# Token attention: maximum, shift and exponential over both units of a turn in one instruction each

## The reference, cut to what matters

```
raw    = einsum('bhid,bhjd->bhij', q, k)
scores = sips_alpha * tanh(raw / sips_beta)
scores = scores + lam * hamming + lat          # bilinear terms of the token's tanh codes
scores = where(causal, scores, -inf)
attn   = softmax(scores, axis=-1)
out    = einsum('bhij,bhjd->bhid', attn, v)
```

## Time and profile before

| what | value |
|---|---|
| median of 3 runs | 4054.79 us (4053.88 to 4055.74) |
| the profiled execution | 4051.72 us |
| its span, first to last instruction | 4049.9 us |
| granted TensorE clock, mean | 0.987 |
| busy share of the span | PE 94%, PEld 72%, DVE 74%, ACT 66%, POOL 48% |
| L400, shift, POOL | 384 instructions, 1039 ns each |
| L469, maximum, DVE | 384 instructions, 674 ns each |
| L587, exponential, ACT | 384 instructions, 662 ns each |

### The profile page before, as it was taken

One profiled execution on the slowest core, in us unless ns is written; L12 is line 12 of the kernel. 1 busy time (PEld: TensorE's weight loads), 2 busy tenths in 40 slices (PEclk: granted clock), 3 DMA queues, 4 the chain that ended last, 5 costly groups with the idle time before them and its releaser, 6 DMA issues. The chain is left out here.

```text
span 4049.9 us, 104259 instructions
## 1 busy us (share of the span) xinstructions
PE 3822.8 (94%) x34969; PEld 2917.7 (72%) x34969; DVE 2984.6 (74%) x7049; ACT 2676.5 (66%) x6409; POOL 1939.4 (48%) x1865
## 2 busy tenths in 40 slices
PE   7999999969999989899999889999999999999999
PEld 5666666647777766577777557777777777789998
DVE  6888888869999965799998665555555555566666
ACT  7888888857778853678787336666666666633333
POOL 4666666657777731566666333334333333311111
PEclk9999999979999999999999999999999999999999
DMA  3000000000000001000000110000000000000000
GB/s 105 1 0 0 0 0 0 0 14 20 20 24 20 24 22 27 14 13 16 13 16 18 24 34 2 1 0 0 0 0 0 0 0 0 0 6 9 9 9 9
DMA packets 69052, 47.65 MB, mean 12 GB/s; under 512 B 38360, under 2 KB 57952, under 8 KB 68832
## 3 DMA queue, kind: packets, MB, share of 16 engines
q1 hardware_dynamic: 68960, 46.43, 4.4%
HBM read 12.62 MB, written 4.19 MB: 4 GB/s over the span
## 5 line engine op out<-in xcount | busy, mean ns | idle before, releaser
L1672 ACT ACTIVATE l_probs<-l_act,l_neg_max 128x128 f32<-128x128 f32 (+1 forms) x1024 | 415.5, 425 | 274.0 <-DVE l_neg_max L1629 271.4
L1609 POOL TENSOR_TENSOR l_probs<-l_probs,l_sums 128x512 f32<-128x512 f32 x384 | 391.0, 1039 | 366.1 <-DVE l_sums L1637 366.1
L400 POOL TENSOR_TENSOR t_probs<-t_probs,t_neg_max 128x512 f32<-128x512 f32 x384 | 390.9, 1039 | 298.6 <-DVE t_neg_max L469 298.4
L1629 DVE TENSOR_REDUCE l_neg_max<-l_act 128x2 f32<-128x512 f32 (+1 forms) x384 | 246.9, 684 | 356.3 <-PE l_act L1728 356.3
L1990 ACT ACTIVATE e_hT<-e_act 128x512 f32<-128x512 f32 x256 | 152.8, 597 | 285.3 <-PE e_act L2011 285.3
L459 DVE SCALAR_TENSOR_TENSOR t_probs<-t_tanh_qk,scalars_sb,t_dve 128x512 f32<-128x512 f32 x384 | 269.4, 743 | 83.6 <-ACT t_tanh_qk L569 52.9
L854 POOL TENSOR_TENSOR w_swappedQ<-w_rawQ,w_table 128x512 f32<-128x512 f32 x128 | 162.1, 1289 | 261.1 <-ACT w_rawQ L1071 261.1
L569 ACT ACTIVATE t_tanh_qk<-t_act,t_inv_beta 128x512 f32<-128x512 f32 x384 | 246.5, 707 | 57.9 <-PE t_act L636 57.7
L2023 PEld LDWEIGHTS e_dve<-e_sb,e_hT 128*128 128x128 f32 x2048 | 268.7, 191 | 13.3 <-ACT e_hT L1990 0.2
L854 POOL TENSOR_TENSOR w_swappedK<-w_rawK,w_table 128x512 f32<-128x512 f32 x128 | 228.6, 1807 | 93.0 <-ACT w_rawK L1071 93.0
L2023 PE MATMUL e_dve<-e_sb,e_hT 128*128 128x128 f32 x2048 | 269.8, 275 | 0.0
(11 more groups left out here) (260 smaller groups left out, 10533.0 us busy)
## 6 DMA issues: line engine op xcount, KB each, us to landing
w_v_mid<-w_v SPq DMA_DIRECT2D x128, 130.0 KB, 2.3
z<-w_z_copy SPq DMA_DIRECT2D x32, 128.0 KB, 2.0
h<-z SPq DMA_DIRECT2D x32, 128.0 KB
out<-x_sb SPq DMA_DIRECT2D x32, 128.0 KB, 1.8
h<-z SPq DMA_DIRECT2D x32, 127.0 KB
wqkv_sb<-L_ffn_wqkv SPq DMA_DIRECT2D x2, 768.0 KB, 6.8
kv_up_sb<-L_attn_w_kv_up SPq DMA_DIRECT2D x1, 1024.0 KB, 9.4
e_sb<-L_ffn_w SPq DMA_DIRECT2D x1, 1024.0 KB, 5.6
```

The source lines that it names most:

```text
L400: nc.gpsimd.tensor_tensor(p, p, neg_max[:, j, 0:len(gs)].unsqueeze(2) .broadcast_to((P, len(gs), P * (t + 1))), ALU.add).then_inc(shifted. ...
L1609: nc.gpsimd.tensor_tensor(p, p, sums[:, at, 0:len(hs)].unsqueeze(2) .broadcast_to((P, len(hs), P * (t + 1))), ALU.mult).then_inc(divided.s ...
L1629: nc.vector.tensor_reduce(neg_max[:, units.index(name), 0:len(hs)], to_act.bank("s" + name, back)[:, :].rearrange("p (h j) -> p h j", h=le ...
L1672: ins = nc.scalar.activation(probs[:, at % SLOTS, s * width:(s + 1) * width], bank[:, s * width:(s + 1) * width], ACT.Exp, bias=neg_max[:, ...
```

## The change

For each turn the pair of instructions on the two units becomes one over both, 1024 columns: the maximum (128 x 4 or 128 x 8 results), the shift, and the exponential. The twins lie in neighbouring slots of `probs`, which `both(i)` returns as one region. The semaphores `maxed`, `shifted` and `exped` count turns and no longer units. Neither the places of these steps in the turns nor any size or ring changes.

```
@@ token_attention
+    def kind(i):
+        gs, t = unit(twins(i)[0])[1:]
+        return len(gs), P * (t + 1)
+        def both(i):
+            return probs[:, 2 * i % SLOTS:2 * i % SLOTS + 2, :]
-        neg_max = sb("neg_max", [P, len(units), 4])
+        neg_max = sb("neg_max", [P, turns, 8])
-        maxed = Count(sem("maxed"), units, [], units)
-        shifted = Count(sem("shifted"), units, [], units)
-        exped = Count(sem("exped"), in_turns(EXP), [], units[:2 * (turns - EXP)], late(EXP))
+        early, over = list(range(turns - EXP)), list(range(turns - EXP, turns))
+        maxed = Count(sem("maxed"), range(turns), [], range(turns))
+        shifted = Count(sem("shifted"), range(turns), [], range(turns))
+        exped = Count(sem("exped"), over + early, [], early, over)
@@ POOL, shift
-                        for name in twins(i) if back else []:
-                            n, gs, t = unit(name)
-                            j = units.index(name)
-                            pool.wait_ge(maxed.sem, maxed.done(name, back))
-                            p = probs[:, j % SLOTS, :].rearrange("p (h j) -> p h j", h=len(gs))
+                        if back:
+                            heads, width = kind(i)
+                            pool.wait_ge(maxed.sem, maxed.done(i, back))
+                            p = both(i).rearrange("p u (h j) -> p (u h) j", h=heads)
                             nc.gpsimd.tensor_tensor(
-                                p, p, neg_max[:, j, 0:len(gs)].unsqueeze(2)
-                                .broadcast_to((P, len(gs), P * (t + 1))), ALU.add).then_inc(shifted.sem, 1)
+                                p, p, neg_max[:, i, 0:2 * heads].unsqueeze(2).broadcast_to((P, 2 * heads, width)),
+                                ALU.add).then_inc(shifted.sem, 1)
@@ DVE, maxima
-                    for name in twins(i):
-                        j, gs = units.index(name), unit(name)[1]
-                        to_dve.wait_drained(dve, "bil" + name, back)
-                        nc.vector.tensor_reduce(
-                            neg_max[:, j, 0:len(gs)],
-                            probs[:, j % SLOTS, :].rearrange("p (h j) -> p h j", h=len(gs)),
-                            AX.X, ALU.max, negate=True).then_inc(maxed.sem, 1)
+                    heads, width = kind(i)
+                    to_dve.wait_drained(dve, "bil" + twins(i)[1], back)
+                    nc.vector.tensor_reduce(
+                        neg_max[:, i, 0:2 * heads], both(i).rearrange("p u (h j) -> p (u h) j", h=heads),
+                        AX.X, ALU.max, negate=True).then_inc(maxed.sem, 1)
@@ ACT, exponential
-                        for name in twins(j) if seq else []:
-                            act.wait_ge(shifted.sem, shifted.done(name, seq))
-                            p = probs[:, units.index(name) % SLOTS, :]
-                            nc.scalar.activation(p, p, ACT.Exp).then_inc(exped.sem, 1)
+                        if seq:
+                            act.wait_ge(shifted.sem, shifted.done(j, seq))
+                            nc.scalar.activation(both(j), both(j), ACT.Exp).then_inc(exped.sem, 1)
@@ PE, transposes
-                    pe.wait_ge(exped.sem, exped.done(name, back))
+                    pe.wait_ge(exped.sem, exped.done(j // 2, back))
```

More of the change, by code:

```diff
@@ L288, in late @@
         return units[2 * (turns - lag):]
-    def in_turns(lag):
-        return late(lag) + units[:2 * (turns - lag)]
     def twins(i):
```

## The result

| | before | after |
|---|---|---|
| median of 6 runs each | 4050.81 us (4045.16 to 4055.74) | 4069.39 us (4064.13 to 4073.89) |
| span of the profiled execution | 4049.9 us | 4067.0 us |
| one period of the token attention (tanh 5 to tanh 5) | 25.17 us | 25.63 us |

The ratio is 1.0045, with a 95% interval of 1.0033 to 1.0058. The forecast was 4070 us and a ratio of 1.0038. The three runs of before that the forecast started from are among the six; their median, 4054.79, lies 4.0 us above that of all six.

What follows compares the result with a forecast made beforehand. It took a loop of waits between PE, ACT and DVE to bound the stage, with POOL's shift close beside. 0.62 - 0.06 - 0.10 = +0.46 us a period, times 30, plus 1.5 at the end, gave +15.3: 4070 us, range 4050 to 4086.

Steps and rivals of the forecast that it cites:

- Step 1: Turn 5: shift 5 ends 0.39 us later, what follows exponential 5 is 0.31 late, and tanh 1 stays in place.
- Steps 2 and 3: Turn 0: shift 0 starts behind the later residual; exponential 0 stalls 0.72 us more, and tanh 2 is 0.62 late.
- Step 4: DVE's sum 2 is 0.62 us late, less 0.06 for maximum 2; copy pT, PE's scores 4 and tanh 4 0.56 late.
- Step 5: Exponential 2 and xn end at 520.55, tanh 4 comes at 520.59: ACT's largest new stall just covered by its PE wait.
- no change: Rival: ACT's new stalls fall into waits it already had; 4052 to 4060 us, chance 0.16.
- Step 6: Exponential 3 has no stall and saves 0.10 us; copy xnT and PE's scores 5 are 0.46 late.
- Faster: Rival: the fixed part of an instruction goes; with a shift of 1.51 us or less, 4047 us; chance 0.13.
- zero point: The joint shift's length at which the change neither gains nor loses, put at 1.66 us.
- Much slower: Rival: the joint shift costs the pair's 2.04 us or more and step 5's cover breaks; 4083 to 4091 us, chance 0.19.

Runs made afterwards that it cites:

- before_center: Kernel before with DVE's center issued ahead of the maxima of turn 2; period 24.70 and 24.71 us (before 25.17), ratios 0.9958 and 0.9959.
- center_late: Changed kernel with center moved behind the sums of turn 3; period 25.78 us (changed kernel 25.63), ratio to before 1.0053.
- shift_halves: Changed kernel with the joint shift split into two instructions of 512 columns; period 26.05 us (changed kernel 25.63), ratio to before 1.0093.
- shift_short: Changed kernel with the joint shift over only seven eighths of each head's columns; period 25.07 us (changed kernel 25.63), ratio to before 0.9995.
- exp_halves: Changed kernel with only the exponential back to one instruction per unit; period 25.88 us (changed kernel 25.63), ratio to before 1.0071.
- center_scalar: Kernel before with center, at its old place, as two one-column instructions with one tensor input each; period 24.88 us (before 25.17), ratio 0.9976.

## Why the prediction was right, point by point

The steps are those of the forecast; the offsets count from tanh 5.

- Prices. Shift 1.89 forecast, 1.895 measured; maximum 1.21 and 1.210; a joint exponential 0.95 to the next start, 0.96 measured (519.32 to 520.28). The broadcast rows were the right ones to draw the line through; the two-operand rows (2.12) were too dear. So was the 2.22, an estimate from the Trainium skill, page "GPSIMD Engine Reference", section 3.1; here the measurement decides.
- Step 1. Tanh 1 stayed (8.48 and 8.49). Exponential 5 waits 0.36 us. Right.
- Steps 2 and 3. Shift 0 behind the residual; exponential 0 starts 2.36 us after tanh 1, where it had been 1.62. I forecast 0.72 more; it was 0.74, and tanh 2 came 0.67 later for 0.62. Sum 2 moved with tanh 2, 0.64 later. Right.
- Step 4 failed. It passed 0.56 us on through DVE to copy pT, and PE's scores 4 came only 0.11 late. I had left center at the 0.55 us that it held DVE before (516.19 to the next sum at 516.74). It was that long because POOL ran the first shift of turn 2 at that time (515.76 to 516.80, center to 516.82; before_center and center_late show it). The joint maximum delays the shift by half a microsecond, so that center slips in ahead of it: 525.67, 0.07 us to the next instruction, shift at 525.83. That gave DVE 0.48 us that no term of the sum had.
- Step 5 took its place. I had exponential 2 and xn ready at 0.52, 0.04 us before PE, and called it just covered. It came 0.57 late and was the last to arrive, since PE was early. That the number stood is in part luck: two chains were of equal length, and when one fell out the other gave the same sum. Had the forecast only had step 4, corrected, it would have said no change (0.62 - 0.06 - 0.48 - 0.10 a period). With step 5 on the path, three shifts and not two set the period, which shift_halves and shift_short confirm.
- Step 6. xnT 0.46 late in the forecast, 0.46 measured, on a path that the forecast had only as its second.
- The sum. Thirty periods made 13.3 us (forecast 13.8). From the first tanh to the first yT it took 1.5 us more, which I had at nothing: the first exponential of all waits 1.05 us for POOL, at 34.44, where it had no wait. The first tanh came 0.4 earlier (29.05 for 29.43). The stage's end took 2.3 more (forecast 1.5). Together that is 16.7 of the 17.1 us between the spans; what stands behind the last yT copy took 0.4 more, far less than its spread over the traces. The medians differ by 18.6, for 15.3 in the forecast. That 4069.39 lies so near 4070 is luck too, since the forecast started 4.0 us too high and was 3.3 too low in the difference.
- The waits. I expected 2.5 to 2.9 us a period of ACT waiting for POOL; it is 2.17, since exponential 2 waits 1.22 and not 1.4, exponential 0 0.61 and not 0.72. The 0.17 and the 0.80 of tanh 1 and tanh 4 for PE did go.
- The rivals. "Faster" would have needed a shift of 1.51 us, and its zero point, forecast at 1.66, lies at 1.72 by shift_short. "Much slower" is shift_halves. That the fixed part saved per instruction would decide was rightly put low: of what was saved on three engines, 66 us of busy time, the loop felt the 0.10 of each of the exponentials 0, 2 and 3 (0.25 us a period by exp_halves) and the 0.145 of each of three shifts (0.42 by shift_halves), and both together were less than the lost overlap. The forecast's 1 us a period that six pairs save on ACT doesn't follow from its own 0.10 a pair, which makes 0.6; ACT's busy time fell by 0.55.

## What to carry to other kernels

Joining two instructions saves their fixed part once, and takes away the overlap of one half with the next engine's work on the other; on this chain of three engines the second was the larger. Before joining, write down for each turn when the joint producer would end and when the consumer is ready, and join only where the first is earlier. And where a small instruction has a strangely long duration, look at what the other engines did in that moment, since a change elsewhere may move it in or out of their way.

## What was not expected of the hardware

Center, a DVE instruction with two tensor inputs from SBUF, does not end, in these traces, while the POOL instruction that was running at its start still runs. Center (128 x 2) ended at 516.82 and 504.58 in two kernels, where the shifts it met ended at 516.80 (515.76 + 1.04) and 504.56; beside an idle POOL it took 0.15 us. It was so every time: in the kernel before, all 30 centers that started beside a shift ended 16 to 18 ns after it, and in center_late all 30 ended 16 to 19 ns after it. With one tensor input (center_scalar) each of the two instructions took 0.20 us in the middle of a shift, and the sums (L459), which read one input from SBUF and one from PSUM, kept their 743 ns beside POOL's shifts. Since the sums are the same operation as center, it is not the operation that waits.

The Trainium skill, page "GPSIMD Engine Reference", section 1, says that POOL shares its SBUF interfaces with VectorE, with contention for DVE instructions with two SBUF inputs or in a 2-port perf mode. The traces agree on the two inputs, and show that the wait lasts to the end of the whole POOL instruction, 0.73 us for work of 0.15.

Other stages of the kernel before show that center is no special case, and that one tensor input is not always enough. First come a DVE instruction of 16 columns with two inputs from SBUF, and POOL beside it. Then comes L193 of DVE on 128 columns, with one tensor input and two numbers per partition, in a stage where POOL runs shifts beside it and in one where POOL is idle:

```profile
947.43 1.12 DVE L945 TENSOR_TENSOR w_lengthsQ<-w_lengthsQ,w_tiny 128x16 f32<-128x16 f32 x1
```

```profile
946.03 2.50 POOL L854 TENSOR_TENSOR w_swappedQ<-w_rawQ,w_table 128x512 f32<-128x512 f32 x2 [3.09 <-ACT w_rawQ L1071]
```

```profile
L193 DVE TENSOR_SCALAR l_xn<-x_sb,l_mv,l_rstd 128x128 f32 x56 | 54.9, 1020 | 0.1
...
L193 DVE TENSOR_SCALAR e_xn<-x_sb,e_mv,e_rstd 128x128 f32 x56 | 16.6, 340 | 0.0
```

L945 takes 1.12 us and ends at 948.55, POOL's pair at 948.53; the two times that POOL was idle beside L945 for Q it took 0.17 and 0.18. L193 takes 1020 ns in the mean beside the shifts and 340 without them. So what center_scalar shows holds for its two instructions of one column and is no rule for one input. Why L193 waits and center_scalar doesn't, no run here shows. Nor does every POOL instruction hold DVE up: L962 of DVE, 1024 columns with two inputs from SBUF, started at 939.82 while POOL ran L867 (937.47 to 940.37) and took 1.21 us, as long as its mean over the kernel, 1.22.
